# One announcement a round instead of three: squaring three matrix exponentials beside a router

## The reference

```
logits = xn @ moe_gate_w + moe_gate_b
topw, topi = top_k(logits, 2)
h = gelu(einsum('bsd,edh->ebsh', xn, ew1) + eb1)
eo = einsum('ebsh,ehd->ebsd', h, ew2) + eb2
moe_out = einsum('ebsd,bse->bsd', eo, w_dense)
for i in range(3):
    moe_out = moe_out @ expm(gens[i])
```

## Time and profile before

| what | us |
|---|---|
| median of three runs | 788.88 |
| lowest and highest run | 787.48, 793.77 |
| span of the profiled execution | 883.8 |
| first squaring to last copy (60.7 to 138.9 in that span) | 78.2 |
| folding of the exponentials into the weights (138.9 to 149.0) | 10.1 |
| first experts (149 to 280, roughly) | 131 |

### The profile page before, as it was taken

How to read it: one execution, slowest core, us unless ns; L and a number is a source line. 1 busy time by engine, 2 the same in 40 slices (tenths; PEclk the granted TensorE clock), 3 DMA queues, 4 the chain that set the end, 5 groups by cost and what they waited for, 6 DMA issues and landing times.

```text
span 883.8 us, 16149 instructions
## 1 busy us (share of the span) xinstructions
PE 683.1 (77%) x4719; PEld 492.3 (56%) x4719; DVE 568.2 (64%) x1922; ACT 410.8 (46%) x931; POOL 485.6 (55%) x588
## 2 busy tenths in 40 slices
PE   1465667979897798997988979999997777838760
PEld 1355656979793354654646545455544466837750
DVE  3675545968767876876767767787673235745538
ACT  2243411545560265664545645556554655615530
POOL 2656554034512666576866768373645466566661
PEclk9968777988898899998999999999997999969985
DMA  8614544744348313023050240302201235233525
GB/s 242 205 48 117 132 123 115 183 112 105 94 113 192 110 31 98 18 65 87 2 130 21 49 103 1 98 17 55 61 13 53 85 78 167 75 93 84 175 96 154
DMA packets 89825, 84.04 MB, mean 95 GB/s; under 512 B 14561, under 2 KB 72556, under 8 KB 89580
## 3 DMA queue, kind: packets, MB, share of 16 engines
q1 hardware_dynamic: 74472, 57.51, 25.8%
q0 software_dynamic: 8800, 19.72, 7.5%
q10 hardware_dynamic: 6468, 5.79, 2.8%
HBM read 43.84 MB, written 31.13 MB: 85 GB/s over the span
## 4 chain that ended last, share of the span: by engine, by line
PE 46%; DVE 15%; another core or an unknown queue 11%; issue 7%; ACT 7%; SPq 5%; ACTq 3%; DMA 3%; POOL 1%; DVEq 0%; POOLq 0%
PE bank L2361 6%; PE bank L2271 6%; PE bank L2401 6%; PE bank L2286 6%; PE bank L2426 6%; SPq L595 4%; DVE mx_of L1923 3%; PE pair L2449 2%; PE bank L2363 2%; ACT beside_parts L1254 2%; DMA qT<-mT_zero 2%; PE pair L2213 2%; PE bank L2246 1%; ACT arena L1326 1%
## 5 line engine op out<-in xcount | busy, mean ns | idle before, releaser
L1326 ACT ACTIVATE arena<-bank 128x512 f32<-128x512 f32 x320 | 184.0, 599 | 175.2 <-PE bank L2401 147.1
L1923 DVE TENSOR_REDUCE mx_of<-bank 128x4 f32<-128x512 f32 x320 | 204.2, 684 | 81.9 <-PE bank L2361 42.9
L2401 PE MATMUL bank<-qT,kZ 128*128 128x512 f32 (+3 forms) x512 | 156.9, 377 | 19.2 <-ACT arena L1326 12.4
L975 POOL TENSOR_SCALAR_AFFINE_SELECT arena<-arena 128x256 f32<-128x256 f32 (+1 forms) x192 | 95.4, 521 | 123.9 <-ACT arena L1326 122.5
L2361 PE MATMUL bank<-kZ,qT 128*128 128x512 f32 x320 | 148.5, 481 | 15.7 <-DVE mx_of L1923 6.2
L2401 PEld LDWEIGHTS bank<-qT,kZ 128*128 128x128 f32 x512 | 95.7, 197 | 49.2 <-ACT arena L1326 24.1
L868 POOL DMA_INDIRECT z_rows<-beside_kZ,place x80 | 78.7, 984 | 51.5 <-DVE place L1685 29.8
L2361 PEld LDWEIGHTS bank<-kZ,qT 128*128 128x128 f32 x320 | 63.1, 200 | 70.7 <-issue 31.4
L885 POOL DMA_INDIRECT sums<-y_rows,y_place x56 | 54.4, 971 | 84.9 <-DMA y_rows<-arena 70.0
L2426 PE MATMUL bank<-arena,vA 128*9 128x512 f32 (+3 forms) x1024 | 92.4, 440 | 5.2 <-POOL arena L975 2.7
L1254 ACT ACTIVATE beside_parts<-bank,hidden_bias 128x128 f32<-128x128 f32 x160 | 45.5, 381 | 69.6 <-remote 44.0
(11 more groups left out here) (286 smaller groups left out, 1306.7 us busy)
## 6 DMA issues: line engine op xcount, KB each, us to landing
arena<-z_rows SPq DMA_DIRECT2D x128, 66.0 KB
qT<-parts SPq DMA_DIRECT2D x42, 128.0 KB
kZ<-parts SPq DMA_DIRECT2D x168, 32.0 KB
y_rows<-arena SPq DMA_DIRECT2D x20, 264.0 KB, 3.3
kZ<-bias_k_r SPq DMA_DIRECT2D x8, 512.0 KB
beside_kZ<-y_rows SPq DMA_DIRECT2D x7, 528.0 KB, 3.9
z_rows<-in_spare SPq DMA_DIRECT2D x4, 528.0 KB
z_rows<-in_spare SPq DMA_DIRECT2D x32, 66.0 KB
```

The costliest lines, as they stand in the source:

```text
L975: g_.affine_select(out=cut, in_=cut, compare_op=ALU.is_ge, fill=0.0, base=0, pattern=[[0, 2], [0, blocks], [1, P]], channel_multiplier=-1) ...
L1326: a_(dst, src, ACT.Exp).then_inc(exp_ok.sem, 1)
L1923: v.tensor_reduce(mx_of[:, queries, :, t, keys], ps_a[n % NA][:, :].rearrange("p (q n) -> p q n", q=NQ), AX.X, ALU.max).then_inc(reduced.s ...
L2401: return mm(outp, kZ[u][:, h, lo:lo + P], qT[u][:, t, lo:SEQ], start=start, stop=True, skip_group_check=(kind != "full"))
```

## The change

TensorE signals `square_pe` once a round, on the second product of r = 2, where it signalled once for each r. VectorE waits once a round, ahead of its copy of r = 0, for the round's number, where it waited ahead of each copy. What TensorE waits for is as it was: the copy of the same r in the round before.

```diff
             def keep_squares(rounds):

                 for i in rounds:
+                    dve.wait_ge(square_pe, i + 1)
                     for r in range(NROT):
-                        dve.wait_ge(square_pe, NROT * i + r + 1)
                         v.copy_predicated(mats[:, r, :, :], over[:, r, i:i + 1].bitcast(U32).unsqueeze(2)
                                           .to_broadcast([P, 2, P]),
                                           banks[r][:, 0:2 * P].rearrange("p (a n) -> p a n", a=2)).then_inc(squared, 1)
...
                         pe.wait_ge(squared, NROT * (i - 1) + r + 2 if i else 1)
                         mm(banks[r][:, 0:P], exp_T[:, r, :], exp_m[:, r, :], start=True, stop=True)
-                        mm(banks[r][:, P:2 * P], exp_m[:, r, :], exp_T[:, r, :], start=True,
-                           stop=True).then_inc(square_pe, 1)
+                        last = mm(banks[r][:, P:2 * P], exp_m[:, r, :], exp_T[:, r, :], start=True, stop=True)
+                    last.then_inc(square_pe, 1)
```

## The result

The changed kernel takes 799.66 us (median of 4 runs, 798.59 to 802.71) beside 791.00 us for the kernel before (4 runs on the same chip, 787.48 to 793.77): ratio 1.0123, 95% interval 1.0087 to 1.0158. So the change costs 6.9 to 12.5 us, about 9.7 by the ratio, where 3.96 were forecast. The time lies inside the range given, by 0.3 us, and the forecast's own mechanism explains less than half of it.

A forecast was written before the change was run, and what follows sets the result against it. The chain of TensorE squaring and VectorE copies, folded into the weights before the experts begin, was taken to set the time. Six times 0.66 us, 3.96 us, on 788.88 gave 792.9 us; range 787.0 to 800.0.

The forecast's parts named there:

- the forecast's own mechanism: In each chunk's third squaring round, all copies come behind TensorE's third pair: 3.96 us added in all, chance 0.62.
- Round c: Third squaring round of a chunk: all three copies, not one, come behind the third pair; 0.66 us added, six times.
- Rounds a and b: First and second squaring rounds of a chunk: later copies hidden by routing and by `abel_logits`; cost nothing.
- Chunk 7's round b: Second squaring round of the last chunk, not covered by `abel_logits`: 0 us at full clock, 1.28 us at half clock.
- a step without a hole: Chunk step without the profile's unknown time: taken to run at full clock, about 7.5 us long.
- The 36 announcements: Announcements and waits dropped in the squaring rounds: taken as 0, with a gain of 1.4 us as the other bound.
- The clock: Rival: longer TensorE pauses before each `ranks` lower its clock, 1.75 us a drop; 803.4 or 796.3 us, chance 0.14.
- What is late next: Behind the last copy, at the experts' start: nothing else is late, so the whole 3.96 us delay passes on.
- GpSimd may fall behind: Rival at GpSimd's sending of chunk rows: experts wait for rows, so squaring is hidden; 0 us, 788.9, chance 0.17.

The follow-up runs named there:

- once_in_a_b: Kernel before with one announcement in each chunk's first and second squaring rounds, three in the third; ratio 0.9990.
- once_in_c: Kernel before with one announcement in each chunk's third squaring round only, three in the first and second; ratio 1.0099.
- once_but_2c: Kernel before with one announcement in the third squaring round of chunks 3 to 7, three in that of chunk 2; ratio 1.0111.
- after_filled: Changed kernel with the four expert-weight transposes behind chunk 2's third squaring round made five times over, filling TensorE's pause ahead of ranks(3); ratio 1.0109 to the kernel before.
- before_delay: Kernel before with 13 chained, unused VectorE instructions, some 4.3 us, between the last copy and the folding of the weights; ratio 1.0100.
- before_again: Kernel before, unchanged, profiled a second time for a profile without holes; 791.28 us, ratio 1.0005.
- before_filled: Kernel before with the four expert-weight transposes behind chunk 3's third squaring round made nine times over, filling TensorE's pause ahead of ranks(4); 786.58 us, ratio 0.9974.
- once_in_2c: Kernel before with one announcement in chunk 2's third squaring round alone, the other 17 rounds as before; ratio 1.0106.
- the moved wait: TensorE's wait for expert bias rows moved to the first product using them: changed kernel 793.43 us, ratio 1.0023; kernel before 789.22 us, ratio 0.9987.

## Why the prediction was wrong

*Round c: right, and the right size.* 0.66 us a step, in chunks 2, 4, 5, 6 and 7 within 0.1 (the table), and 0.80 in chunk 3 with the clock nearly as it was (11.72 against 10.92). In chunk 4 the agreement is luck: its step varies by more than that between kernels that are alike there. Six of them are the 3.96 us (which with 788.88 make 792.8, not 792.9).

*Rounds a and b: right.* Hidden, by once_in_a_b. Chunk 7's round b cost nothing either, at full clock. The reason given, that a step without a hole runs at full clock, does not hold: chunk 4's step runs in part at the low one in both kernels.

*The 36 announcements: right at nothing.* In chunk 2's round c, the first product of r = 2 begins 0.22 us behind the last of r = 1 in the kernel before, where an announcement stands between them (62.74 and 62.96), and 0.23 us behind it in the changed kernel, where none does (62.82 and 63.05). The 26 ns for each that the Trainium skill gives ("TensorE: Matmul & The Clock Gate", section "The cost: per-tile semaphore tail") were not there to be saved.

*The clock: a rival that came true in one step of six.* The prediction named the longer pause, put it at up to 1.2 us, and priced a drop at 1.75 us. The pause that decided was 2.16 us, ahead of `ranks(3)`, where VectorE has one more instruction to do between the last copy and `gate_logits` (L1456, 0.55 us); the drop cost 1.5 to 2.0 us. In chunks 5 to 7 pauses of about 1.2 us left the clock at 1.00, and in chunk 4 it was low already. The rival's price had the forecast in it, but it was worked out for six drops and for two; with the one that came, 3.96 + 1.75 = 5.7 us, it fits the steps (5.8 us by the sums). The mistake was the pause in chunk 3, which the estimate of 1.2 us for a clean step missed; it is the smaller part of the miss.

*"What is late next": the step that failed.* It looked at the experts' tiles and at GpSimd's sending, found them ahead, and concluded that "the delay passes on whole". It did not: the last copy moved by 5.9 us and the experts' start by 10.3, with a wait of 6.0 us that the prediction put at nothing. It passed over ScalarE's three DMAs of bias rows, which are issued only as the weight copies of the folding begin (111.13 and 111.14), and which the experts wait for at once. Before the change these were in time by a hair: the third was issued 0.6 us ahead of SyncE's second transfer. The bias rows then moved by 5.90 us with the squaring (111.13 to 117.03), the transfer by 4.55 only (113.22 to 117.77): 0.6 ahead became 0.75 behind. The transfer waits in the code for GpSimd's sending of a chunk's rows, which runs back to back, 1.27 us for each DMA, and lags: its last one moved by 2.0 us (121.18 to 123.12). Before the change the transfer goes when, by the count, GpSimd's rows for it have just landed (the last sent at 110.91, a median of 2.5 us to land). Afterwards these (the last sent at 112.94) should have landed by 115.4, and it goes 2.3 us later, 5.6 us behind the first transfer. It waited for those rows still, by the view of SyncE's waits in the changed kernel from 100 to 120 us:

```profile
SPq L607 <- DMA z_rows<-beside_kZ,place: 5.2, 1, 5.2
```

So the rows took 4.8 us to land, beside the first transfer of 512 KB (issued at 112.14); that this transfer held them was not tried. The prediction noted that GpSimd may fall behind, as a reason for no cost at all; but what does not move along with the squaring can change its order with what does. In each profile in which the third bias row was issued behind the transfer the experts waited (changed kernel, once_in_c, once_but_2c, after_filled, before_delay), for 1.5 to 6.1 us; in each in which it was ahead they started 0.1 to 0.8 us behind the last weight copy (before_again, before_filled, once_in_a_b, once_in_2c).

Together: 5.8 us in the steps (3.96 of round c and the drop of the clock) and 6.0 in the wait, less the 1.6 us by which the folding of before was slowed by its own low clock: 10.2 us at the experts' start, counted from chunk 2's `gate_logits` (58.98 and 69.19), and 9.7 (6.9 to 12.5) in the time. Shown in the time are round c as the origin (once_in_c against once_in_a_b) and the wait (the moved wait). The clock's share is shown in the profiles alone. Open is once_in_2c and its time. The profiled execution took 787.77 us, its bias rows just in time, the other three 792.88 to 799.26. A margin of half a microsecond that is kept in some executions and lost in others would explain it, but that is not shown: the others left no profile.

## What to carry to other kernels

One announcement in place of three takes away the overlap of the consumer with the producer's later pieces: here it was free only where the consumer came later anyway, and there it brought nothing either. When a chain is delayed, list every transfer that is issued at its end and is waited for at once, and compare its issue with that of large transfers on other queues, which may not move along; a margin of half a microsecond is none. And a pause that grows can cost a second time through the clock, in the next step.

## What the hardware showed that was not expected

With two DMAs of 512 KB issued among them on another queue, three DMAs of 2.1 KB were through only between 122 and 126 us, and what waits for them started 6.6 us behind the end of the last issue (119.16 to 125.80); issued ahead of those, they were through within 1.2 us of it (113.26 to 114.5). A pause of TensorE of 1.24 us left the clock at full level behind it and one of 1.90 us or more in the same place didn't; one of 4.2 us or more ahead of `ranks(4)` lowered it in every profile looked at, unless it was filled. The Trainium skill has this for pauses between bursts ("TensorE: Matmul & The Clock Gate", section "HAM oscillation — how this bites in real kernels"); the runs agree, and filling the pause of 4.2 us with 32 transposes won 0.26%.
